# Attention and experts in one program: the first expert block is fixed from 13 chunks and run inside the tail of the attention phase

## The reference, cut to what matters

```python
for i in range(2):                                   # "attention"
    n = layer_norm(x) * w[i] + b[i]
    kv = (n @ Wk.T) * (n @ Wv.T); r = sigmoid(n @ Wr.T)
    state_t = 0.95 * state_{t-1} + 0.05 * kv_t       # over the 2048 positions
    x = x + (r * state) @ Wo.T
x = layernorm(h + x)
top_v, top_i = top_k(x @ Wg.T, 2); probs = softmax(top_v)
for e in range(8):
    out += probs_e * ((silu(x @ W1[e].T) * (x @ W2[e].T)) @ W3[e].T)
x = layernorm(x + out)
```

## Time and profile before

| | |
|---|---|
| median of 3 runs | 1187.16 us (1185.73 to 1188.01) |
| the profiled execution | 1190.37 us, of which the profile's span is 1188.5 us |
| busy share: TensorE, VectorE, GpSimd, ScalarE | 91%, 76%, 56%, 53% |
| mean granted TensorE clock | 0.961 |
| attention's last matmul of step 18 | at about 508.6 us |
| first expert block's hidden products begin | at 520.62 us |
| last expert matmul | at about 1131 us |
| rest: last adding, second norm | to 1188.5 us |

### The profile page before, as it was taken

One profiled execution on the slowest core, in us unless ns is written; L12 is line 12 of the kernel. 1 busy time (PEld: TensorE's weight loads), 2 busy tenths in 40 slices (PEclk: granted clock), 3 DMA queues, 4 the chain that ended last, 5 costly groups with the idle time before them and its releaser, 6 DMA issues. The chain is left out here.

```text
span 1188.5 us, 22060 instructions
## 1 busy us (share of the span) xinstructions
PE 1083.6 (91%) x6624; PEld 956.2 (80%) x6624; DVE 898.0 (76%) x1986; ACT 625.8 (53%) x1079; POOL 662.6 (56%) x560
## 2 busy tenths in 40 slices
PE   6999999999999998759999999999999999999900
PEld 6778888888888887647888889888889999999900
DVE  5778888888888886647766667777776777888737
ACT  4445555555555553345445545655654665666528
POOL 1111544545454553667677657676774666777434
PEclk9899999999999999869999999999999999999965
DMA  4011221111121211357666557777886787989469
GB/s 160 18 54 53 54 55 54 54 53 53 53 53 53 63 44 37 89 148 203 151 167 162 124 141 191 220 196 182 220 210 147 186 233 210 264 238 256 96 197 386
DMA packets 80242, 164.33 MB, mean 138 GB/s; under 512 B 27568, under 2 KB 44976, under 8 KB 79920
## 3 DMA queue, kind: packets, MB, share of 16 engines
q1 hardware_dynamic: 49968, 127.72, 33.7%
q0 software_dynamic: 30208, 35.81, 17.0%
HBM read 118.78 MB, written 44.70 MB: 138 GB/s over the span
## 5 line engine op out<-in xcount | busy, mean ns | idle before, releaser
L1195 POOL DMA_INDIRECT x_acc<-fy_sb,pair_out x136 | 256.0, 1882 | 129.9 <-issue 52.1
L1385 PE MATMUL fring<-fxh,fw_hi 128*128 128x256 f32 (+1 forms) x704 | 234.9, 334 | 8.0 <-DVE fxl L1299 5.6
L1387 PE MATMUL fring<-fxh,fw_lo 128*128 128x256 f32 (+1 forms) x704 | 233.5, 332 | 0.0
L1386 PE MATMUL fring<-fxl,fw_hi 128*128 128x256 f32 (+1 forms) x704 | 232.7, 331 | 0.0
L1215 ACT ACTIVATE fw_hi<-w_raw 128x1024 fp32r<-128x1024 f32 x156 | 163.5, 1054 | 88.7 <-PE fy L1430 79.6
L1277 DVE TENSOR_TENSOR fw_lo<-w_raw,fw_hi 128x1024 fp32r<-128x1024 f32 x156 | 189.5, 1219 | 12.5 <-ACT fw_hi L1215 11.8
L98 POOL DMA_INDIRECT xg<-x_src,pair_in x136 | 154.6, 1137 | 71.2 <-issue 39.0
L559 POOL TENSOR_TENSOR rs<-ve,neg_half 128x4 f32<-128x4 f32 x48 | 55.7, 1160 | 238.7 <-DVE nm L646 238.6
L88 POOL DMA_INDIRECT slot_list<-pairs,slot_u x128 | 135.8, 1061 | 51.0 <-issue 35.0
L884 PE MATMUL ring<-xh,w_hi 128*128 128x512 f32 x384 | 160.4, 418 | 2.0 <-issue 1.9
L1428 PE MATMUL fy<-fw_hi,gh 128*128 128x256 f32 x544 | 155.9, 287 | 0.0
(11 more groups left out here) (149 smaller groups left out, 2021.6 us busy)
## 6 DMA issues: line engine op xcount, KB each, us to landing
w_raw<-w_ffn SPq DMA_DIRECT2D x156, 512.0 KB, 5.0
x_in<-h SPq DMA_DIRECT2D x16, 512.0 KB, 3.2
x_src<-x SPq DMA_DIRECT2D x16, 512.0 KB, 4.3
x_acc<-x SPq DMA_DIRECT2D x16, 512.0 KB, 5.9
acc<-x_acc SPq DMA_DIRECT2D x16, 512.0 KB, 7.3
out<-o SPq DMA_DIRECT2D x16, 512.0 KB, 6.4
xg<-x_src,pair_in POOLq DMA_INDIRECT x136
x_acc<-fy_sb,pair_out POOLq DMA_INDIRECT x136
```

What stands on the lines that cost most here:

```text
L1195: nc.gpsimd.indirect_dma_start(x_acc, bass.IndirectOffsetOnAxis(pair_out[j][:, q, 0:1].bitcast(U32), 0), y[j][:, q, :], None, compute_op=A ...
L1385: nc.tensor.matmul(out, hi, rows_hi, start=dc == 0, stop=False)
L1386: nc.tensor.matmul(out, hi, rows_lo, start=False, stop=False)
L1387: last = nc.tensor.matmul(out, lo, rows_hi, start=False, stop=dc == DC - 1)
```

## The change

- `EARLY` is 13: the big blocks are fixed one chunk earlier. This gives 18 big blocks, 9 singles and 27 pairs: 54 blocks and 135 tiles. The order starts with 8 big blocks (`FRONT`) instead of 10 before the singles, and one big block stands between the last single and the pairs.
- The attention and expert programs are one (`attention_and_experts`), so no meeting of all engines lies between them. The attention steps end at 16. What steps 17 to 19 did is written into the expert steps -1 to 5: the last chunk's `output2`, the transposes, gates, ranks, choices, places, shares, scatters and stores.
- `big_table` moves from VectorE's step 16 end to its step 16 start, ahead of `residual2`. `first_block` moves to SyncE's step 16, and its gather to right behind GpSimd's step 16. In that step GpSimd issues all eight scatters of chunk 12 ahead of `rstd(2)`; before it issued two, `rstd(2)`, then six.
- The first block's weights are split in step 16 (parts 0 and 1) and in expert step 0 (part 2).
- `gap` has two buffers. The shares of the last two chunks are worked out together in expert step 1, after the Silu table was loaded in step -1; they use Sigmoid. Their scatters go in expert steps 2 to 5, four in each.
- Some expert buffers share memory with attention buffers that are dead by then. One more DMA zeroes the last chunk's rows of `x_src` at the start.
- More expert steps are unrolled: -1 to 11, loop 12 to 23, 24 to 31, loop 32 to 49, 50 to 55.

```diff
-EARLY = CHUNKS - 2
+EARLY = CHUNKS - 3
-SINGLES = E
+SINGLES = E + 1
-SIZES = [Q] * 10 + [Q, 1] * SINGLES + [Q] * (BIG - SINGLES - 10) + [2] * PAIRS
+FRONT = 8
+SIZES = [Q] * FRONT + [Q, 1] * SINGLES + [Q] * (BIG - SINGLES - FRONT) + [2] * PAIRS
...
-        LAST = CHUNKS + 4
+        LAST = CHUNKS + 1
...
             def first_block():
...
                 for i, (low, high) in enumerate(PART):
                     sp.dma_start(w_raw_all[:, low:high], ...).then_inc(kept.s_w[i][0], 16)
+                store(CHUNKS)
                 for par in range(2):
-                    sp.wait_ge(s_st[par], 32 * (EARLY // 2))
-                    sp.wait_ge(s_sc[par], SCAT * (EARLY // 2))
+                    chunks = (EARLY + 1 - par) // 2
+                    sp.wait_ge(s_st[par], 32 * chunks)
+                    sp.wait_ge(s_sc[par], SCAT * chunks)
                 sp.dma_start(kept.pair_in[0][:, :, :], ...)
...
-                if at(s, CHUNKS + 1):
+                if at(s, CHUNKS):
                     first_block()
...
+            def xstep(s, half, j, spot):                       # SyncE
+                if at(s, -1):
+                    pairs(spot, 2, pair_in, 1, s_pair[1])
+                if at(s, 0):
+                    sp.wait_ge(s_padst, 64)
+                    store(CHUNKS + 1, 1)
+                if at(s, FRONT - 2):
+                    sp.wait_ge(kept.s_table, 6)
+                    for par in range(2):
+                        sp.wait_ge(s_st[par], 32 * (CHUNKS // 2))
+                        sp.wait_ge(s_sc[par], SCAT * (CHUNKS // 2))
...
+                if at(s, CHUNKS):                              # ScalarE, attention step 16
+                    w_half(0, 0, 0, 0, Spot(-1), 1)
+                    w_half(1, 0, 0, 0, Spot(-1), 1)
...
+                if at(s, 0):                                   # ScalarE, expert step, after unit 1
+                    normalize3(CHUNKS + 1, CHUNKS // 2, 1)
...
+                if at(s, 1):                                   # ScalarE, end of the step
+                    probs(CHUNKS + 1, CHUNKS // 2, 1)
+                    probs(CHUNKS + 2, CHUNKS // 2 + 1, 0)
...
-                    scatter(s, j, 0, 2)                        # GpSimd, step 16
+                    scatter(s, j, 0, 8)
                     rstd(2, s - 2)
-                    scatter(s, j, 2, 6)
...
+                if at(s, -1):                                  # GpSimd, behind the gather of block 1
+                    open_scatter(CHUNKS + 1, CHUNKS // 2, 1)
+                    scatter_pairs(nc, kept, slot_list, 1, 0, 4)
+                    rstd(2, CHUNKS - 1)
+                    scatter_pairs(nc, kept, slot_list, 1, 4, 4)
...
+                if isinstance(s, int) and 2 <= s <= 5:
+                    scatter_pairs(nc, kept, slot_list, s // 4, s % 2 * Q, Q)
...
             run(pool, step)
+            gather_rows(nc, pool, kept, x_src, f_met, 0, 0, Q)
+            run_experts(pool, xstep)
...
+                if at(s, EARLY + 3):                           # VectorE, ahead of residual2
+                    dve.wait_ge(s_base, EARLY + 1)
+                    big_table(nc, dve, kept)
                 if at(s, CHUNKS):
                     residual2(s, j)
+                    norm_stats(2, z, s - 2)
...
+                if at(s, -1):                                  # VectorE, expert steps
+                    residual2(CHUNKS + 1, 1)
+                    frows_lo(spot, 1)
+                    norm_stats(2, z, CHUNKS - 1)
+                    choose(CHUNKS - 2, 1)
+                    return
...
+                if at(s, 0):
+                    place(CHUNKS - 2, CHUNKS // 2, 1)
+                if at(s, 1):
+                    choose(CHUNKS - 1, 0)
...
                         hidden(s, j, u, spot)                  # TensorE, expert steps
+                        if at(s, 0) and u == 1:
+                            rank_products(CHUNKS + 1)
+                        if at(s, 0) and u == 2:
+                            rows3(CHUNKS + 2, 0, f_xl, spot.before(ROW_BANKS, 1))
+                        if at(s, 1) and u == 1:
+                            rank_products(CHUNKS + 2)
...
+                if at(s, -1):
+                    gates(CHUNKS + 1, s_slot, CHUNKS - 2)
+                if at(s, 0):
+                    gates(CHUNKS + 2, s_slot, CHUNKS - 1)
...
             run(pe, step)
+            rows3(CHUNKS + 1, 1, s_xl[1], 2 * CHUNKS)
+            output2(CHUNKS + 1, 1)
+            run_experts(pe, xstep)
```

More of the change, by code:

```diff
@@ L384, in _, with first_row, pairs @@
-            run(sp, step)
+                elif within(s, 2, CHUNKS):
+                    store(s, j)
+            run(sp, step)
+            def first_row(which, spot, d, bound):
+                n, kind = spot.column(d)
+                column = n + KIND_FIRST[kind]
+                columns = slice(column, column + 1) if isinstance(column, int) else bass.ds(column, 1)
+                return sp.value_load(table[0:1, which, columns], min_val=0, max_val=bound)
+            def pairs(spot, d, dst, j, done):
+                tiles = spot.size(d)
+                row = first_row(1, spot, d, SLOTS - CH)
+                return sp.dma_start(dst[j][:, 0:tiles, :], slot_list[bass.ds(row, tiles * P), :]
+                                    .rearrange("(p q) c -> p q c", p=P)).then_inc(done, 16)
@@ L451, in normalize3, with probs, w_half @@
                 normalize(2, z, x1[:, j, :, :], s - 2, s_x1)
+            def probs(s, half, j):
+                act.wait_ge(s_gap, s - 2)
+                if within(s, 5, CHUNKS + 2):
+                    act.wait_ge(s_sc[1 - j], (half - 2 + j) * SCAT)
+                nc.scalar.activation(pairs[1 - j][:, :, 0, 1], gap[:, 1 - j, :], ACT.Sigmoid)
+                nc.scalar.activation(pairs[1 - j][:, :, 1, 1], gap[:, 1 - j, :], ACT.Sigmoid, scale=-1.0).then_inc(s_prob, 1)
+            def w_half(i, b, half, j, spot, d):
+                low, high = PART[i]
+                act.wait_ge(f_w[i][j], half * 16 + 16)
+                if within(b, 2, BLOCKS):
+                    if i < 2:
+                        act.wait_ge(f_h, spot.before(UNITS, d - 1) * 2)
+                    else:
+                        act.wait_ge(f_y, spot.before(OUT_BANKS, d - 1))
+                nc.scalar.activation(fw_hi[j][:, low:high], fw_raw[:, j, low:high], ACT.Copy).then_inc(f_whi[i], 1)
             split_weights(0)
@@ L514, in step @@
                 if within(s, 3, CHUNKS + 2):
[L515 to L519, removed]
+                    probs(s, half, j)
+                if at(s, CHUNKS):
+                    w_half(0, 0, 0, 0, Spot(-1), 1)
+                    w_half(1, 0, 0, 0, Spot(-1), 1)
                 if layer2:
@@ L827, in step, with gate @@
                     gated(dve, 1, s - 1, 0)
-                if at(s, EARLY + 2):
-                    dve.wait_ge(s_base, EARLY + 1)
-                    big_table(nc, dve, kept)
                 if layer2 and not at(s, CHUNKS):
                     recur(1, s - 1, 1, j)
+            def gate(b, u, spot):
+                v = spot.before(UNITS, 0) + u
+                dve.wait_ge(f_h, v * 2 + 2)
+                dve.wait_ge(f_silu, v + 1)
+                if u >= 2 or within(b, 1, BLOCKS):
+                    dve.wait_ge(f_gl, v if u == 0 and spot.size(-1) == 1 else v - 1)
+                nc.vector.tensor_tensor(fgated[:, u % 2, :], ring[2 * (u % 2) + 1][:, :], silu[:, u % 2, :],
+                                        ALU.mult).then_inc(f_g, 1)
@@ new lines, in weigh @@
+            def weigh(half, j, spot):
+                tiles = spot.size(-1)
+                dve.wait_ge(f_pair_out[j], half * 16 + 16)
+                for k in range(OUT_BANKS[tiles]):
+                    bank, n = ((j + PAIR_TURN) % 2 if tiles == 2 else k), min(tiles, 2)
+                    dve.wait_ge(f_y, spot.before(OUT_BANKS, -1) + k + 1)
+                    share = pair_out[j][:, 2 * k:2 * k + n, 1:2].bitcast(F32).to_broadcast([P, n, D])
+                    nc.vector.tensor_tensor(fy[j][:, 2 * k:2 * k + n, :], out1[bank][:, 0:n, :], share, ALU.mult).then_inc(f_yv, 1)
@@ L930, in gates, with rank_products @@
                 last.then_inc(s_g, 1)
+            def rank_products(s):
+                pe.wait_ge(s_picked, s - 2)
+                ranks = out1[0][:, 0, RANK_AT:RANK_AT + Q * E]
+                flat = picked[:, :, :].rearrange("p q e -> p (q e)")
+                nc.tensor.matmul(ranks, before[:, :], flat, start=True, stop=False)
+                for d in range(1, Q):
+                    nc.tensor.matmul(ranks[:, d * E:Q * E], ones[:, :], flat[:, 0:(Q - d) * E], start=False, stop=d == Q - 1)
+                for q in range(Q):
+                    last = nc.tensor.matmul(out1[0][:, 0, RANK_AT + Q * E:RANK_AT + Q * E + E], ones[:, :],
+                                            picked[:, q, :], start=q == 0, stop=q == Q - 1)
+                last.then_inc(s_rank, 1)
             bias_products(0, (0,))
```

(1 more changed line is left out.)

636 lines of the change are left out of this document (284 added, 352 removed).

## The result

The changed kernel takes 1182.16 us (median of 6 runs, 1180.75 to 1182.31); the kernel before took 1187.59 in the runs beside it. The ratio is 0.9943, with a 95% interval of 0.9918 to 0.9969: 5.4 us faster where 19.6 were forecast. The profiled executions differ by more, 1188.5 - 1180.3 = 8.2 us of span, since the one of before lay 3.2 us above its median, with four pair periods of 9.6 to 10.2 us in a row, three of them between the two rows 998.42 and 1028.15.

What follows compares the result with a forecast made beforehand. TensorE was taken to bind outside the hole between attention and experts, a chain of waits inside it. 17.4 us from the handover plus 2.2 from the block mix made 19.6 off 1187.2: 1167.5 us, 80% range 1160 to 1180.

Steps and rivals of the forecast that it cites:

- The handover's first half: From attention's end to the first expert block: block 0's first product starts at 498.4, 22.2 us earlier.
- The list: Block 0's pair list, issued by SyncE at about 484.2, was taken to need 3 us to land, between 2 and 5.
- The low clock: TensorE at half clock around block 0: transposes to first product 3.5 us, then 1.0 us allowed within block 0's 16.4.
- Step 1: Expert step 1: TensorE stands 3.0 us, plus 0.3 of ranks and 1.0 of low clock; 4.3 lost, 17.4 left.
- The mix: Expert blocks: two big blocks less, one single and three pairs more, a gain of 2.2 us.
- VectorE's queue: Rival, chance 0.14: VectorE binds the first two blocks, 6.9 us less gain, 1174.5 us.
- Slow pairs: Rival, chance 0.14: pair periods slow down from 9.09 us; at 9.5 the kernel takes 1178.7 us.
- The merge gives nothing: Rival, chance 0.03: block 0's gather comes no earlier, only the block mix's gain is left, 1185 us.
- The better case: Chance 0.07: list lands in 2 us, no low clock, pairs at 8.93; 7 us more gain, 1160.5 us.

Runs made afterwards that it cites:

- the fourth run: The changed kernel with the last chunk's rank products one unit later in TensorE's order, after block 1's third unit: 1176.34 us, ratio 0.9882.
- runs 6: The kernel before with SBUF gaps putting only the hidden products' rows at -128 bytes from the weights modulo 4096: 1193.16 us beside a median of 1191.6.
- run 13: The kernel before plus a measuring stage of hidden and output products at 11 operand distances, results thrown away; its whole time says nothing.
- run 14: The changed kernel with later rank products, block 2's weights loaded early and SBUF gaps, the first gap 128 bytes instead of 320: 1170.55 us, ratio 0.9818.
- run 10: The changed kernel with later rank products, two SBUF gaps, and two parts of block 2's weights loaded ahead of the last store: 1163.33 us, ratio 0.9764.
- run 11: The kernel of run 10 plus 14 useless filling products on TensorE between the last output and block 0's transposes: 1165.56 us, ratio 0.9776.
- run 7: The changed kernel with later rank products and SBUF gaps of 320 bytes before the expert weights and 64 before the gated halves: 1163.84 us, ratio 0.9761.

## Why the prediction was wrong

**The handover's first half was right, in its order and nearly in its times.** Table ready at 469.95 (forecast 470.7), GpSimd's scatters done at 478.8 (479.0), the norm of chunk 14 from 480.3 (480.3), output at 488.65 (488.8), list issued at 483.97 (484.2). The list took 4.2 us to the first gather, not 3, and the rows were there at 496.1, not 494.9.

**The low clock was sized too small.** From transposes to first product I took 3.5 us at a mostly full clock; it was 5.0 at the lower one, with gates of 3.42 us instead of about 1.85 in between. So the first product came at 501.1, not 498.4. Block 0 then took 17.2 instead of 16.4: 3.6 us of the gain missing by block 1.

**Step 1 was the right mechanism with too small a price.** The stand was 3.48 us (forecast 3.0), and behind it twelve products took 533.15 - 527.89 = 5.3 us instead of 12 x 0.2325 = 2.8: 2.5 us of low clock where I took 1.0, though I had written 2.3 as the upper end. The rule cited there from the Trainium skill's page TensorE: Matmul & The Clock Gate (Part 1), that an idle TensorE falls to half clock and needs sustained work to regain it, agrees with the trace: the clock is 0.52 in the window 526 to 533 and 1.00 behind it. The price of up to 2.3 was 0.2 short. From block 1's transposes to block 2's it was 20.3 us against 13.7 before. That the stand was the cause is shown by the fourth run, which took it away by moving one call and gained 7 us by the ratios. Moving the call is no sure cure: two of three profiles with it keep a stand of over 2 us. 17.4 us was forecast for block 2, 11.6 came, and the version with later ranks, gaps and early weights has its transposes at 529.45, 18.1 us earlier than before.

**The mix was the step that failed.** Its term in the sum was 2.2 us of gain and came out as 3.5 us of loss, half of what is missing; the other half lies in the steps above, most of it low clock. It took 17.32 for granted as the price of a large block, because the products are the same. The price belongs to where the operands lie. This was on view in the diff, which turns `fw_hi` into two tensors and puts others between; I read it as bookkeeping and costed it at nothing without a word. Seven large periods by 0.47 and nine of a large and a single by 0.37 ((852.52 - 692.33)/7 = 22.88 against 22.51) make 6.6 us, and with the mix's own -2.2 and 0.9 less for 27 pairs at 9.06 instead of 9.09 it is 3.5, as measured. (That 9.06 is close to 9.09 is chance: before, most pairs took 8.93 and four of them about 10, after, nearly all took 9.01.) Against what the same kernel does with the gaps it is 14 us, since the pairs gain too. Shown three ways: by addresses put into the kernel before (the loss), by gaps in the changed one (the gain), and by the streams alone. With the gaps alone the ratio of 0.9822 puts the kernel at about 1166 us, next to the forecast, but that is luck: block 2 is as late as in the changed kernel, and the pairs at 8.77 give back what is lost there.

**The rivals.** VectorE's queue bound block 1 by 0.5 us more than I had it, no more. Slow pairs: false, (1107.82 - 899.52)/23 = 9.06 a period. The merge gives nothing: false, at 11.6 us. The better case was closed by the low clock and by the list's 4.2 us.

**The best version** is the change with gaps and later ranks: 0.9761, about 28 us less than before at its level. Early weights and fillings add nothing to it.

**Still open.** Why some pair periods are 8.62 and others 8.92 with the same distances; why the output products of large blocks lost 0.2 us when their own distance had not changed (in runs 6 and 14); and why a shorter stand with early weights did not shorten the whole. The first two look alike: at a distance of 64 bytes a stream of 256 columns runs in one kernel at either of two speeds, a pair's 48 hidden products in 5.44 or 5.65 us (113 or 118 ns each), a large block's 48 output products in 5.54 or 5.74. It looks as if the distance only decides which speeds are to be had; what decides between the two is isolated by no run here.

## What to carry to other kernels

A price read off a trace belongs to the addresses of its operands as well as to the instruction: when a change moves allocations, compare the distance between starts of the same matmuls before and after, first of all, and try a gap of 64 to 320 bytes before looking for a cause in the program. Read a table like that of run 13 for every width of matmul that the kernel has; run 14 shows what it costs not to. A stand of TensorE costs its length and the half clock behind it (here 3.5 and 2.5 us), so where work of another stage is interleaved, put its products on TensorE one unit later than the engine that feeds them seems to need, and look into more than one profile whether the stand is gone. And filling a stand is worth only what the next wait lets through.

## What the runs showed of the hardware that was not expected

- In the sweep a stream of matmuls with 512 moving columns takes 228 to 234 ns each and with 256 columns 114 to 120 ns, by the distance in SBUF between the moving and the stationary operand; the two widths have different best distances (0 and 256 bytes for 512 columns, 64 and 320 for 256).
- At the same distance of 64 bytes a pair's hidden products of 256 columns took 113 ns each in one block and 118 in the next (run 10).
- Copying by ScalarE and subtracting by VectorE in SBUF, beside 20 of the 24 streams of the second round, changed these figures by at most 0.5 ns in all but one that can be compared.
- After a stand of 3.7 us the clock stayed at its lower level through 9.5 us in which TensorE was busy 9.41 us with transposes, gates and products (0.50 in that window); after a stand of 0.52 us it stayed at the upper one (run 11). A stand of 2.27 us was enough to bring it down: in run 7 the stand ended at 530.42, and the clock was 1.00 from 527 to 530 and 0.50 from 533 to 535.
